# Softmax attention on one core: TensorE's steps in double gaps, inverse sums turned into rows, two buffers for pair results

## What is computed

```python
q = (x @ Wq).reshape(b, n, 16, 64)          # b 8, n 512, 16 heads of 64
k, v = 4 heads each of x @ Wkv              # one key/value head serves 4 query heads
q = q * cos + rotate_half(q) * sin          # k likewise
attn = softmax(q @ k.T / 8)
x1 = layernorm(x + (attn @ v).reshape(b, n, 1024) @ Wo + bo)
```

## Time and profile before

| | us |
|---|---|
| median of 3 runs | 3483.9 |
| lowest and highest | 3481.72, 3492.31 |
| profiled execution | 3476.33 |
| its span (first to last instruction) | 3474.6 |
| TensorE busy in the span | 2916.5 (84%) |
| VectorE, ScalarE, GpSimd busy | 2036.1, 1343.6, 963.2 |
| mean granted TensorE clock | 0.914 of full speed |

### The profile page before, as it was taken

One profiled execution on the slowest core, in us unless ns is written; L12 is line 12 of the kernel. 1 busy time (PEld: TensorE's weight loads), 2 busy tenths in 40 slices (PEclk: granted clock), 3 DMA queues, 4 the chain that ended last, 5 costly groups with the idle time before them and its releaser, 6 DMA issues. The chain is left out here.

```text
span 3474.6 us, 61109 instructions
## 1 busy us (share of the span) xinstructions
PE 2916.5 (84%) x16442; PEld 2043.2 (59%) x16443; DVE 2036.1 (59%) x3929; ACT 1343.6 (39%) x2751; POOL 963.2 (28%) x1303
## 2 busy tenths in 40 slices
PE   6999898989989857877999999969888888837993
PEld 4565565656556536765777777744444445416992
DVE  3656565565656537764665656557566666635664
ACT  3545454544545422212222222215444444424443
POOL 3434342333424112113333333310111111121225
PEclk8999999999999978988999999979888898968996
DMA  2111111111111120120000000023211121124225
GB/s 66 32 26 37 34 28 31 29 38 25 37 28 28 28 72 31 36 100 19 13 12 12 12 12 12 7 65 78 61 50 53 54 55 54 43 67 158 73 73 189
DMA packets 190113, 163.02 MB, mean 47 GB/s; under 512 B 85754, under 2 KB 153490, under 8 KB 189330
## 3 DMA queue, kind: packets, MB, share of 16 engines
q1 hardware_dynamic: 178836, 138.40, 14.5%
q0 software_dynamic: 6912, 18.96, 1.4%
q10 hardware_dynamic: 4224, 4.19, 0.3%
HBM read 87.73 MB, written 37.06 MB: 36 GB/s over the span
## 5 line engine op out<-in xcount | busy, mean ns | idle before, releaser
L1120 ACT ACTIVATE soft_probs<-soft_ps_s,soft_mx 128x512 f32<-128x512 f32 x512 | 354.7, 693 | 413.1 <-DVE soft_mx L1042 400.7
L1042 DVE TENSOR_REDUCE soft_mx<-soft_ps_s 128x1 f32<-128x512 f32 x512 | 346.3, 682 | 247.0 <-PE soft_ps_s L952 205.8
L1844 DVE TENSOR_REDUCE mla_mx<-mla_ps_s 128x1 f32<-128x512 f32 x512 | 334.4, 685 | 240.4 <-PE mla_ps_s L1704 216.4
L1947 ACT ACTIVATE mla_pt<-mla_ps_t 128x512 f32<-128x512 f32 x512 | 292.0, 600 | 396.0 <-PE mla_ps_t L1716 356.7
L961 PE MATMUL soft_ps_p<-ident,soft_probs 128*128 128x128 f32 x2048 | 326.0, 283 | 68.7 <-ACT soft_probs L1120 45.6
L952 PE MATMUL soft_ps_s<-soft_ks,soft_qs 128*128 128x512 f32 x1024 | 373.9, 447 | 0.0
L961 PEld LDWEIGHTS soft_ps_p<-ident,soft_probs 128*128 128x128 f32 x2048 | 245.2, 144 | 189.8 <-DVE soft_mx L1042 98.5
L970 PE MATMUL soft_ps_a<-soft_pt,soft_v 128*64 128x512 f32 x1024 | 284.3, 635 | 24.1 <-DVE soft_ri L1046 15.6
L1052 DVE COPY soft_pt<-soft_ps_p 128x512 f32<-128x512 f32 x256 | 176.2, 688 | 137.3 <-PE soft_ps_p L961 135.4
L1704 PE MATMUL mla_ps_s<-mla_stack,mla_pad 128*128 128x512 f32 x512 | 234.7, 465 | 24.2 <-DVE mla_mx L1844 19.1
L1716 PE MATMUL mla_ps_t<-mla_shifted,mla_pad 128*128 128x512 f32 x512 | 223.8, 439 | 29.6 <-ACT mla_pt L1947 27.0
(11 more groups left out here) (334 smaller groups left out, 6609.2 us busy)
## 6 DMA issues: line engine op xcount, KB each, us to landing
soft_rrep<-inverse SPq DMA_DIRECT2D x128, 128.0 KB, 3.1
mla_pad<-mla_stack SPq DMA_DIRECT2D x256, 64.0 KB, 2.0
moe_xt<-by_expert SPq DMA_DIRECT2D x72, 129.0 KB, 2.0
soft_ks<-soft_ks SPq DMA_DIRECT2D x64, 128.0 KB, 2.4
raw<-in_L_ffn_w SPq DMA_DIRECT2D x16, 512.0 KB, 8.2
mla_stack<-mla_yh SPq DMA_DIRECT2D x128, 64.0 KB, 2.1
soft_xc<-in_L_attn_x SPq DMA_DIRECT2D x8, 512.0 KB, 4.7
soft_xb<-in_L_attn_x SPq DMA_DIRECT2D x8, 512.0 KB, 4.0
```

Source lines behind the costliest of these rows:

```text
L1042: op = vv.tensor_reduce(out=mx[:, h, t:t + 1], in_=ps_s[:, s_bank(4 * h + t), :], axis=AX.X, op=ALU.max, negate=True)
L1120: op = nc.scalar.activation(probs[:, h % 2, t, :], ps_s[:, s_bank(4 * h + t), :], ACT.Exp, bias=mx[:, h, t:t + 1], scale=1.0, accum_out=rs ...
L1844: op = vv.tensor_reduce(out=mx[:, a, t, s:s + 1], in_=ps_s[:, (16 * a + 4 * t + s) % S_BANKS, :], axis=AX.X, op=ALU.max, negate=True)
L1947: op = nc.scalar.activation(pt[:, t % 2, s, :], ps_t[:, s % 2, :], ACT.Exp, scale=KPH ** -0.5)
```

## The change

- TensorE's steps of two gaps are merged into one double gap and sorted: P, then transposes (RT, T, QT, KT), then A, then S, then Q, KV and W. So P P, A A and S S stand together. The scores start at gap 32. All places are given anew: P(h, c) stands three double gaps behind S(h, c).
- RT (new) turns the two heads' `ri` (128x8) into 8 rows of 128 in PSUM; RC (new) on ScalarE copies them to `rrow`; RW writes these rows. RW waits for RC, RR for RW. RW is in gap S0 + 8p + 13, O(p) in S0 + 8p + 18.
- `ot` has two buffers; O(p) waits for OL(p - 2). OH(0) and OL(0) move to gap 60, those of pair 1 to 62.
- F writes into `xb` instead of `r`, N and ST follow; LB waits for the four stores and moves to the start of the body, XB to gap 8.
- S waits for the turned q of its own block and half alone, not for all.

```diff
-        rrep = sb("rrep", [P, SEQ])
-        ot = sb("ot", [P, SEQ])
+        rrep, rrow = sb("rrep", [P, SEQ]), sb("rrow", [P, P])
+        ot = sb("ot", [P, 2, SEQ])
-        r = sb("r", [P, 2, D])
...
-        stored = [sem(f"stored{s}") for s in range(2)]
+        stored = sem("stored")
...
-        ROUND, S0 = 4 * HEADS, 36
+        ROUND, S0 = 4 * HEADS, 32
...
-        attend = lambda p, c: S0 + 8 * p + (10, 12, 14, 15)[c]
-        for g in range(ROUND):
-            h, c = g // 4, g % 4
-            put(S0 + g + 5, "tensor", ("P", h, c))
-            put(S0 + g + 5, "scalar" if c % 2 else "vector", ("E", h, c))
-        for g in range(ROUND):
-            h, c = g // 4, g % 4
-            put(S0 + g, "tensor", ("S", h, c)); put(S0 + g, "vector", ("M", h, c))
-            if c == 3:
-                put(S0 + g + 2, "vector", ("I", h))
+        for h in range(HEADS):
+            for c in range(TT):
+                at = S0 + 4 * h + c // 2 * 2
+                put(at + 6, "tensor", ("P", h, c)); put(at + 6, "scalar" if c % 2 else "vector", ("E", h, c))
+                put(at, "tensor", ("S", h, c)); put(at + 1, "vector", ("M", h, c)); put(at + 1, "scalar", ("X", h, c))
+            put(S0 + 4 * h + 6, "vector", ("I", h))
+            at = S0 + 8 * p
-                put(attend(p, c), "tensor", ("A", p, c))
-            at = attend(p, TT - 1) + 1
-            put(at, "vector", ("O", p)); put(at, "gpsimd", ("OH", p), ("OL", p))
-            put(S0 + 8 * p + 10, "sync", ("RW", p), ("RR", p))
-        def project(at, u):
-            put(at, "tensor", u)
-            put(at + 1, "vector", ("ROT",) + u, *([("VC", u[1])] if u[0] == "KV" else []))
-            put(at + 1, "gpsimd", *((n,) + u for n in ("Y0", "Y1", "HI", "LO")))
-        def turn_over(at, key):
-            put(at, "tensor", key); put(at, "scalar", ("C",) + key)
+                put(at + 12 + c // 2 * 2, "tensor", ("A", p, c))
+            put(at + 12, "tensor", ("RT", p)); put(at + 12, "scalar", ("RC", p)); put(at + 13, "sync", ("RW", p), ("RR", p))
+            put(at + 18, "vector", ("O", p)); put(at + (28, 22, 18)[min(p, 2)], "gpsimd", ("OH", p), ("OL", p))
+        def project(d, u):
+            put(2 * d, "tensor", u)
+            put(2 * d + 2, "vector", ("ROT",) + u, *([("VC", u[1])] if u[0] == "KV" else []))
+            put(2 * d + 2, "gpsimd", *((n,) + u for n in ("Y0", "Y1", "HI", "LO")))
+        def turn_over(d, *keys):
+            for key in keys:
+                put(2 * d, "tensor", key); put(2 * d, "scalar", ("C",) + key)
-        for t, at in enumerate((2, 5, 8, 11)):
-            project(at, ("KV", t))
-        for t, (at, back) in enumerate(((14, 18), (17, 22), (21, 26), (25, 29))):
-            project(at, ("Q", 0, t))
-            for b in range(2):
-                turn_over(back + b, ("QT", 0, t, b))
-        for g, at in enumerate((16, 20, 28, 40)):
-            turn_over(at, ("KT", g)); put(at + 1, "sync", ("KD", g))
-        for t, (at, back) in enumerate(((33, (37, 38)), (39, (43, 44)), (45, (52, 57)), (47, (58, 59)))):
-            project(at, ("Q", 1, t))
-            for b in range(2):
-                turn_over(back[b], ("QT", 1, t, b))
-        put(31, "gpsimd", ("VV", 0)); put(46, "gpsimd", ("VV", 1))
-        put(63, "gpsimd", ("XB",)); put(63, "sync", ("LB",))
-        for t, at in enumerate((48, 50, 53, 55)):
-            at += ROUND
-            put(at, "tensor", ("W", t, 0)); put(at + 1, "tensor", ("W", t, 1))
+        for t, d in enumerate((1, 2, 4, 5)):
+            project(d, ("KV", t))
+        for g, d in enumerate((8, 10, 12, 17)):
+            turn_over(d, ("KT", g)); put(2 * d + 1, "sync", ("KD", g))
+        for (half, t), (d, back) in {(0, 0): (6, 9), (0, 1): (8, 11), (0, 2): (9, 13), (0, 3): (12, 15), (1, 0): (13, 16), (1, 1): (16, 19), (1, 2): (17, 20), (1, 3): (21, 24)}.items():
+            project(d, ("Q", half, t))
+            turn_over(back, *turned(("Q", half, t)))
+        put(24, "gpsimd", ("VV", 0)); put(40, "gpsimd", ("VV", 1))
+        put(ROUND + 2, "sync", ("LB",), ("LX",)); put(ROUND + 8, "gpsimd", ("XB",))
+        for t, d in enumerate((24, 25, 28, 29)):
+            at = ROUND + 2 * d
+            put(at, "tensor", ("W", t, 0), ("W", t, 1))
-        put(ROUND + 2, "sync", ("LX",))
-        for g in range(ROUND):
-            h, c = g // 4, g % 4
-            put(S0 + g, "scalar", ("X", h, c))
+        turn = {"P": 0, "RT": 1, "T": 1, "QT": 1, "KT": 1, "A": 2, "S": 3, "Q": 4, "KV": 4, "W": 4}
+        for d in range(0, ROUND, 2):
+            gaps[d, "tensor"] = sorted(gaps.get((d, "tensor"), []) + gaps.pop((d + 1, "tensor"), []), key=lambda k: turn[k[0]])
...
-                   "QT": lambda k: (act_s, ("C",) + k), "KT": lambda k: (act_s, ("C",) + k), "W": lambda k: (dve_s, ("F", k[1]))}
+                   "RT": lambda k: (act_s, ("RC", k[1])), "QT": lambda k: (act_s, ("C",) + k), "KT": lambda k: (act_s, ("C",) + k), "W": lambda k: (dve_s, ("F", k[1]))}
...
-                for s in range(2):
-                    sp.sem_inc(stored[s], 32)
+                sp.sem_inc(stored, 16 * TT)
+                sp.sem_inc(inverse_out, 16)
...
                     elif kind == "LB":
-                        hold(sp, *dve_s.at(i, "F", TT - 1))
-                        sp.dma_start(xb[:, :, :], batch(x_in, index + 1)).then_inc(xb_loaded, 16)
+                        hold(sp, stored, 16 * TT * i[0] + (16 * TT * i[1] + 16 * TT))
+                        sp.dma_start(xb[:, :, :], batch(x_in, index)).then_inc(xb_loaded, 16)
...
-                        hold(sp, *dve_s.at(j, "I", 2 * p + 1))
+                        hold(sp, *act_s.at(j, "RC", p))
-                        sp.dma_start(inverse.rearrange("s (t p) -> p s t", p=P), ri[:, 2 * p:2 * p + 2, :], allow_slow_non_contiguous=True).then_inc(inverse_out, 16)
+                        sp.dma_start(inverse.rearrange("s (t p) -> (s t) p", p=P), rrow[0:2 * TT, :]).then_inc(inverse_out, 16)
-                        hold(sp, inverse_out, 128 * j[0] + (128 * j[1] + 16 * p + 16))
+                        hold(sp, inverse_out, 128 * j[0] + (128 * j[1] + 16 * p + 32))
-                        sp.dma_start(x_out[bass.ds(index, 1), P * t:P * t + P, :].rearrange("o p d -> p (o d)"), r[:, t % 2, :]).then_inc(stored[t % 2], 16)
+                        sp.dma_start(x_out[bass.ds(index, 1), P * t:P * t + P, :].rearrange("o p d -> p (o d)"), xb[:, t, :]).then_inc(stored, 16)
...
-                sp.dma_start(xb[:, :, :], batch(x_in, 0)).then_inc(xb_loaded, 16)
-                for key in [("LX",)] + [k for k in ahead["sync"] if k[0] != "LB"]:
+                for key in [("LX",)] + ahead["sync"]:
...
-                for s in range(2):
...
+                        elif kind == "RT":
+                            p = key[1]
+                            pe.wait_ge(*dve_s.at(j, "I", 2 * p + 1))
+                            last = nc.tensor.transpose(m[0:2 * TT, 0:P], ri[:, 2 * p:2 * p + 2, :].rearrange("p s t -> p (s t)"), ident[:, :])
...
-                            if h % HH == 0 and t == 0:
-                                pe.wait_ge(*act_s.at(j, "C", "QT", h // HH, TT - 1, 1))
+                            if h % GRP == 0:
+                                pe.wait_ge(*act_s.at(j, "C", "QT", h // HH, t, g % 2))
...
-                            dve.wait_ge(*(pool_s.at(j, "OL", p - 1) if p else pool_s.at(shift(j, -1), "OL", PAIRS - 1)))
-                            op = vv.tensor_tensor(ot[:, :], ps_a[:, 0, :], rrep[:, :], ALU.mult)
+                            dve.wait_ge(*(pool_s.at(j, "OL", p - 2) if p >= 2 else pool_s.at(shift(j, -1), "OL", PAIRS + p - 2)))
+                            op = vv.tensor_tensor(ot[:, p % 2, :], ps_a[:, 0, :], rrep[:, :], ALU.mult)
-                            dve.wait_ge(stored[t % 2], 32 * j[0] + (32 * j[1] + 16 * (t // 2) + 32))
-                            op = vv.tensor_tensor(r[:, t % 2, :], ps_m[:, bank["W", t], 0:D], xb[:, t, :], ALU.add)
+                            op = vv.tensor_tensor(xb[:, t, :], ps_m[:, bank["W", t], 0:D], xb[:, t, :], ALU.add)
...
+                        elif kind == "RC":
+                            p = key[1]
+                            act.wait_ge(*pe_s.at(j, "RT", p))
+                            act.wait_ge(inverse_out, 128 * j[0] + (128 * j[1] + 16 * p + 16))
+                            op = nc.scalar.copy(rrow[0:2 * TT, :], ps_m[0:2 * TT, bank["RT", p], 0:P])
...
-                            op = nc.gpsimd.tensor_copy(ath[:, p, :], ot[:, :])
+                            op = nc.gpsimd.tensor_copy(ath[:, p, :], ot[:, p % 2, :])
-                            op = nc.gpsimd.tensor_tensor(atl[:, p, :], ot[:, :], ath[:, p, :].bitcast(F32), ALU.subtract)
+                            op = nc.gpsimd.tensor_tensor(atl[:, p, :], ot[:, p % 2, :], ath[:, p, :].bitcast(F32), ALU.subtract)
```

6 lines of the change are left out of this document (3 added, 3 removed).

## The result

The changed kernel takes 3387.05 us (median of 4 runs, 3384.29 to 3392.99), the kernel before beside it on the same chip 3482.81 (4 runs, 3479.19 to 3492.31). The ratio is 0.9732, with a 95% interval from 0.9715 to 0.9748: faster by 2.7%. The profiled execution took 3384.29 us, its span 3382.5, which is 92.1 less than before. 85.5 of these lie in the first stage, whose last W starts at 1190.6 us in place of 1276.2; the other 6.6 lie in stages that the change doesn't touch.

What follows compares the result with a forecast made beforehand. TensorE was taken to set the time, busy 140 of a body's 153 us. The terms -69 - 10 - 14 + 13 - 20 + 3 = -97 us gave 3379 profiled, 3387 as median; range 3350 to 3440.

Steps and rivals of the forecast that it cites:

- forecast A: Whole kernel: the forecast itself, a change of -60 to -130 us; chance 0.62.
- Part 1: First stage, order on GpSimd and two ot buffers: TensorE's stop and half-speed stretch go, 9.8 us per body, -69 us.
- Part 5: Inverse sums as rows: waits in the last batch and half-speed stretches shrink, -20 us, bounds 0 and -28.
- Part 2: Order of TensorE's products: A in pairs saves at its edges, RT costs some; -1.5 us per body, -10 us.
- Part 3: Latencies with double gaps: 2.8 us of small waits go, 0.8 come back; -2 per body, -14 us.
- Part 4: Turn of the loop: VectorE's stays 7.6 us, the cost rises from 7.7 to 9.9; +2.2 per turn, +13 us.
- Part 6: First batch: QT(1,0) ahead of the first S makes TensorE wait for the chain through one rt; +3 us.
- 0.8 back: Loop body: waits of 0.8 us per body that return where double gaps leave the scores' PSUM banks too little time.
- B: Whole kernel: the turn and waits between double gaps take part back, about -50 us (3434); chance 0.16.
- E: Whole kernel: something of the same size replaces the stop, so time stays within 0.3%; chance 0.05.
- C: Double gaps: S(n+3) waits for its bank in each, making the kernel slower, +37 us (3521); chance 0.07.
- D: Loop branches: another body length or place changes the turns, giving 3328 or 3438 us; chance 0.05.

Runs made afterwards that it cites:

- b_oh: The kernel before, with only OH and OL of pair 0 moved from gap 52 to 58, behind the last W; ratio 0.9905 to the kernel before.
- b_ohrows: b_oh plus the inverse sums written as rows (RT, RC, RW one gap later), gaps still single; ratio 0.9784 to the kernel before.
- a_odd18: The changed kernel with query projections and the turnings of queries and keys in other double gaps, OH and OL unmoved; ratio 0.9589 to the kernel before.
- a_alt: The changed kernel with P A S P A S in each double gap instead of P P A A S S; ratio 0.9996 to the kernel before.
- a_dummy: The changed kernel plus an element-by-element write of 128 x 8 bias values to scratch at each body's end; ratio 0.9873 to the kernel before.

## Why the prediction came true, and where it did so by luck

The time was predicted to 0.1 us, forecast A holds. The terms were not that good, and that the number fits so closely is luck: the profiled execution was to take 3379 us and took 3384.3, and the median was taken 7.6 us above it, where it came out 2.8 above. These two errors of 5 us cancel. Predicted and measured by the same cuts, in us of the first stage:

| | predicted | measured |
|---|---|---|
| Part 1, order on GpSimd (b_oh) | -69 | -41 |
| Part 5, rows of inverse sums (b_ohrows) | -20 | -38 |
| Parts 2, 3, 4, 6, double gaps (changed less b_ohrows) | -8 | -6 |
| stage | -97 | -85 |

The remaining 6.6 of the span, in stages that were not touched, made the sum look better than it was. The rows do not match the parts one to one: what the edit of Part 5 did to the turn of Part 4 stands in its row. The two `ot` buffers were not measured apart: they have no effect of their own in b_oh, which does without them, and I ran no kernel with them alone.

**Part 1: mechanism right, size off by its surroundings.** The stop, N's 11 us and one of the two stretches at half speed are gone, as written. The step that failed is a silent one, that nothing else would come in its place on TensorE. In b_oh QT waits about 2 us a body for W's bank, 12.3 of the 22 us that six periods lack; the 0.5 us that I counted as an aftermath stayed, and the clock gave back two thirds of what I took. In the changed kernel, with its other order of products, that bank wait is gone. TensorE's own branch, 4.2 us in half of b_oh's turns and in all of the changed kernel's, is new as well, but it is not where Part 1 lost: b_oh's periods with the slow branch are the shorter ones.

**Part 2: right in sign, too small.** The order of the products takes 4.2 us off TensorE's busy time in a body (136.0 to 131.8) and the eight RT add 1.2: -3.0 where I took -1.5. A pair of A gains 0.15 us against the old order where nothing else stands beside it; the rest I did not follow step by step. a_alt's 0.35 per pair is the price of its own order, not what the change won.

**Part 3: here a step failed outright.** I went through the copies by what they compute ("QT now stands three or more double gaps behind its projection") and left out whose bank they take. The bank of QT' belongs to the projection of the double gap before, whose rotation waits for the single `rt`, on which GpSimd is late. "0.8 back" was 6.4 us of waits for `rt` (3.4, 2.2, 0.8), and a stretch at half speed behind them. With the short waits for v and for `qs` it makes 7.0 us a body outside the turn, where I had 0.8. a_odd18, which differs from the changed kernel by the places of the projections and turnings alone, and so by the order of `ps_m`, is 5.7 us per body and 48 us in the stage faster: that is what the step was worth.

**Part 4: wrong premise, and its error paid for Part 3's.** I took VectorE's turn of 7.6 us as given. It was that long with the write of `ri` in flight, which the same change removes; the turn fell to 2.8. Its cost to TensorE fell from the 9.9 that I wrote to 1.9 for its own branch, 0.3 to 2.2 for the exponential of the first S, and a clock stretch in some turns: about 4. "At the turn TensorE waits 5 to 6 us for VectorE's copy into `pt`" is wrong; a_dummy, with such a write put back, shows that wait as 4.94. So +2.2 a body became some -4, 6 us better than forecast, while Part 3 came out 6 us dearer than its -2 (2.8 us of small waits gone, 7.0 new).

**Part 5: -20 in the last part is -21.** The write of 8 rows takes 0.9 us where I took 3.1, so only 3.4 us are left ahead of the last products, not 5. The effect on the loop, -16, was not in the sum.

**Part 6.** The first part grew by 2.1 us (+3). Inside it QT and KT wait for `rt` as in the loop.

**The rivals.** B (the turn takes part back, 3434) and E (nothing moves) did not come. C, the bank chain, was priced at the wrong bank: I feared the three banks of `ps_s`, which show 0.3 us in the body of the rows above and 10.3 in the whole stage, and never asked about the two of `ps_m`. D, branches of another length or place, did happen, on another engine than I looked at: TensorE's branch went from 0.22 to 4.29 us. Where TensorE waits for it alone, that is 1.9 us; in b_oh no cost of it shows. The Trainium skill, "Runtime: NRT & Kernel Launch", section Instruction fetch mechanics, says that a taken branch whose target is outside the two pages at hand has to fetch it first. By that rule, the traces agree that the slow turn is a fetch: one instruction queue (q8) moved 38 packets in the kernel before, 65 in b_oh, 93 in the changed kernel, nine more for each slow turn. Why the same 998 instructions fetch at no turn in one kernel and at every second in the other, no run here settled.

## What to carry to other kernels

When a schedule by hand moves steps, follow for each step not only its inputs but the buffer that it writes: with n buffers in turn, the product n places before must have been *read*, and what reads it may hang on an engine two links away. One list of the order with its banks found all four places; the profile shows them as a wait for a tensor that the waiting step does not use (QT for `rt`). A transfer of single elements costs more than the wait for it: look at what else goes on meanwhile, the turns of loops first. When bodies alternate, cut them a second time at another place before you blame what stands at the cut: cut at the branch, b_oh's slow turns seem to cost 6 us, cut in mid-body they cost nothing. And a sum that comes out right proves none of its terms; experiments that each do one part were what showed two errors of 6 us per body against each other.
